# Two transformer layers in one kernel: the order of the first loads, and scales that TensorE spreads over the partitions

## What is computed

```python
x = x + fake_quant(layernorm(x)) @ fake_quant(ctx)      # uint8 grids, ctx is 2 x 1024 x 1024
x = x + attention0(layernorm(x))                         # 32 heads, 8 key/value heads, rotary, biases bq, bk, bv
x = x + experts0(layernorm(x))                           # 64 experts of rank 16, top 16
x = x + neighbours(ctx, layernorm(x))                    # 16 nearest of 1024 points, weights affine_w, affine_b
x = x + attention1(layernorm(x))                         # causal, output projection
x = x + experts1(layernorm(x))                           # 8 experts, top 1

def fake_quant(x, scale, zp):                            # scale and zp are one number each
    return (clip(round(x / scale + zp), 0, 255) - zp) * scale
```

## Time and profile before

| | |
|---|---|
| device time, median of 3 runs | 268.38 us (268.18 to 269.42) |
| the profiled execution's own time | 268.93 us |
| span of the profile, first to last instruction | 267.1 us |
| busy: PE / VectorE / ScalarE / GpSimd | 216.7 / 197.6 / 78.6 / 24.0 us |
| chain that ended last, share of the span | PE 47%, VectorE 31%, ScalarE 9%, transfers 4%, GpSimd 4% |
| bytes moved | 44.88 MB, 168 GB/s on average |

### The profile page before, as it was taken

How to read it: one execution, slowest core, us unless ns; L and a number is a source line. 1 busy time by engine, 2 the same in 40 slices (tenths; PEclk the granted TensorE clock), 3 DMA queues, 4 the chain that set the end, 5 groups by cost and what they waited for, 6 DMA issues and landing times.

```text
span 267.1 us, 4882 instructions
## 1 busy us (share of the span) xinstructions
PE 216.7 (81%) x2107; PEld 140.9 (53%) x2107; DVE 197.6 (74%) x356; ACT 78.6 (29%) x120; POOL 24.0 (9%) x34
## 2 busy tenths in 40 slices
PE   0419999899969398779966995698978999897983
PEld 0214447345758276564435444697966475654561
DVE  3759888999976999989999796958781135861433
ACT  1279962100282456545107103000001021430010
POOL 4155931000000000010000001000001000000010
PEclk9999999999997559599999999689999999999999
DMA  2699999980065059457739575000079000000002
GB/s 59 229 415 410 412 410 356 336 347 5 0 176 140 4 163 306 158 167 328 303 116 415 211 301 221 2 5 2 5 253 376 2 0 2 2 0 2 0 0 79
DMA packets 17435, 44.88 MB, mean 168 GB/s; under 512 B 2364, under 2 KB 7614, under 8 KB 16391
## 3 DMA queue, kind: packets, MB, share of 16 engines
q1 hardware_dynamic: 16256, 43.90, 45.2%
q10 hardware_dynamic: 1158, 0.69, 0.9%
HBM read 43.99 MB, written 0.59 MB: 167 GB/s over the span
## 4 chain that ended last, share of the span: by engine, by line
PE 47%; DVE 31%; ACT 9%; DMA 4%; POOL 4%; issue 3%; ACTq 1%; DVEq 0%; POOLq 0%; SPq 0%
PE banks L360 8%; PE banks L375 7%; PE banks L648 6%; PE banks L428 5%; PE banks L612 5%; ACT bufZ L688 4%; DVE bufY L1212 3%; POOL arc L1321 3%; DVE knn_d L938 3%; DVE idx L933 3%; DVE idx L946 3%; DVE v L942 3%; DMA ring<-in_ctx 3%; DVE v L929 3%; PE banks L287 3%
## 5 line engine op out<-in xcount | busy, mean ns | idle before, releaser
L287 PE MATMUL banks<-cst 128*128 128x256 bf16 (+1 forms) x182 | 22.2, 274 | 0.7 <-ACT arc L712 0.7
L360 PE MATMUL banks<-are,xnT 128*128 128x512 f32 (+1 forms) x64 | 21.7, 492 | 0.7 <-ACT xnT L816 0.7
L929 DVE MAX8 v<-banks 128x8 f32<-128x1024 f32 x16 | 19.5, 1219 | 3.0 <-PE banks L281 3.0
L287 PEld LDWEIGHTS banks<-cst 128*128 128x128 bf16 (+1 forms) x182 | 17.9, 103 | 6.3 <-issue 4.2
L1308 POOL TENSOR_SCALAR veps<-mv 128x1 f32<-128x1 f32 x6 | 1.3, 221 | 217.4 <-DVE mv L915 217.4
L816 ACT COPY xnT<-banks 128x512 f32<-128x512 f32 x8 | 4.3, 589 | 52.7 <-PE banks L300 52.7
L942 DVE MAX8 v<-knn_d 128x8 f32<-128x1024 f32 x16 | 19.6, 1223 | 0.2
L933 DVE FIND_INDEX8 idx<-v,banks 128x8 uint32<-128x1024 f32 x16 | 19.6, 1223 | 0.0
L317 PE MATMUL banks<-cst,ring 128*128 128x128 f32 x96 | 16.7, 331 | 3.5 <-ACT ard L712 2.9
L946 DVE FIND_INDEX8 idx<-v,knn_d 128x8 uint32<-128x1024 f32 x16 | 19.5, 1218 | 0.0
L1212 DVE COPY_PREDICATED bufY<-hi_mask,banks 128x256 f32<-128x256 uint8 (+1 forms) x40 | 15.3, 388 | 5.6 <-PE banks L648 4.4
(11 more groups left out here) (191 smaller groups left out, 357.0 us busy)
## 6 DMA issues: line engine op xcount, KB each, us to landing
ring<-in_ctx SPq DMA_DIRECT2D x4, 1024.0 KB, 9.9
are<-in_L_attn_wq SPq DMA_DIRECT2D x1, 4096.0 KB, 26.1
ring<-in_L_ffn_A SPq DMA_DIRECT2D x4, 1024.0 KB, 13.4
are<-lo_scratch SPq DMA_DIRECT2D x4, 1024.0 KB, 7.3
ard<-in_L_attn_Wq SPq DMA_DIRECT2D x1, 4096.0 KB, 13.9
ring<-lo_scratch SPq DMA_DIRECT2D x4, 1024.0 KB, 4.6
arc<-in_L_attn_Wo SPq DMA_DIRECT2D x1, 4096.0 KB, 13.8
ard<-in_ctx SPq DMA_DIRECT2D x3, 1024.0 KB, 16.5
```

Of the source, the lines that this page charges most:

```text
L287: mm(bank[bk][low:P, 0:2 * P], idle_pat[:, low:P], idle_pat[:, :], start=True, stop=True)
L360: m = mm(o, xnTk[:, k, :], w(k), start=(l == 1 and k == 0), stop=(k == KT - 1))
L929: v.max(v8[:, 0, :], dist_ps[:, :]).then_inc(sem("max_done"), 1)
```

## The change

Five edits. ScalarE issues the constants, x, and the four numbers, now each as a single element into a row of four on partition 0 (`scale_row`); the biases and the two affine loads move to SyncE, behind the context and ahead of the weights. SyncE queues the context when the constants have landed, and no longer waits for the points and the numbers. PE multiplies the row of ones by the row of four ahead of its first transposes, which puts the four numbers on all 128 partitions in PSUM, and VectorE copies them into `scal` before the quantiser's scalars. VectorE's order in the search changes: second_max(0), first_max(1) and second_index(0) come before the sums. The three `wsel` operations move from before the context product to after `advance(3)`.

```diff
--- before.py
+++ after.py
@@ -126,6 +126,7 @@
         veps = sb("veps", [P, 1])
         bperm = sb("bperm", [P, 2 * HALF])
         onesr = bufY[0:1, 1536:1536 + P]
+        scale_row = bufY[0:1, 1536 + P:1540 + P]
         xout = bufX[:, 0:D]
 
         ident = cst[:, C_ID:C_ID + P]
@@ -214,10 +215,13 @@
                 b, k, n = CHUNKS[i]
                 load(ctx_chunk(i).rearrange("p (k n) -> p k n", k=n), ctx_v[b, :, k:k + n, :], f"ld_ctx{i}")
 
-            sp.wait_ge(sem("ld_xy"), 32)
-            sp.wait_ge(sem("ld_scal"), 64)
+            sp.wait_ge(sem("ld_cst"), 16)
             for i in range(len(CHUNKS)):
                 load_ctx(i)
+            for n, (o, w) in (("L0_attn_bq", (0, D)), ("L0_attn_bk", (D, DKV)), ("L0_attn_bv", (D + DKV, DKV))):
+                load(bufY[0:1, o:o + w], A[n].unsqueeze(0), "ld_bias")
+            load(scal[:, 4:20], A["L1_xattn_affine_w"].partition_broadcast(P), "ld_affine")
+            load(scal[:, 20:21], A["L1_xattn_affine_b"].partition_broadcast(P), "ld_affine")
             for n, (o, w) in (("L0_attn_wq", (0, D)), ("L0_attn_wk", (D, DKV)), ("L0_attn_wv", (D + DKV, DKV))):
                 load(W0[:, :, o:o + w], A[n].rearrange("(k p) n -> p k n", p=P), "ld_" + n[-2:])
             sp.wait_ge(sem("ctx_quant"), 5)
@@ -529,6 +533,9 @@
                         dist(10)
 
 
+            pe.wait_ge(sem("ones_set"), 1)
+            pe.wait_ge(sem("ld_scal"), 64)
+            mm(bank[4][:, 0:4], onesr[:, :], scale_row, start=True, stop=True).then_inc(sem("scal_spread"), 1)
             pe.wait_ge(sem("ld_cst"), 16)
             pe.wait_ge(sem("feat_ones"), 3)
             pe.wait_ge(sem("feat_sq"), 2)
@@ -761,13 +768,9 @@
                 act.dma_start(dst, src).then_inc(sem(name), 16)
 
             load(cst[:, :], A["consts"], "ld_cst")
+            load(x[:, :], A["x"].rearrange("b s d -> (b s) d"), "ld_x")
             for i, n in enumerate(("L0_xattn_x1_scale", "L0_xattn_x1_zp", "L0_xattn_x2_scale", "L0_xattn_x2_zp")):
-                load(scal[:, i:i + 1], A[n].partition_broadcast(P), "ld_scal")
-            load(x[:, :], A["x"].rearrange("b s d -> (b s) d"), "ld_x")
-            for n, (o, w) in (("L0_attn_bq", (0, D)), ("L0_attn_bk", (D, DKV)), ("L0_attn_bv", (D + DKV, DKV))):
-                load(bufY[0:1, o:o + w], A[n].unsqueeze(0), "ld_bias")
-            load(scal[:, 4:20], A["L1_xattn_affine_w"].partition_broadcast(P), "ld_affine")
-            load(scal[:, 20:21], A["L1_xattn_affine_b"].partition_broadcast(P), "ld_affine")
+                load(scale_row[:, i:i + 1], A[n].unsqueeze(0), "ld_scal")
 
             def evac_points(b, i):
 
@@ -1073,7 +1076,8 @@
 
             def quantiser():
 
-                dve.wait_ge(sem("ld_scal"), 64)
+                dve.wait_ge(sem("scal_spread"), 1)
+                link(v.tensor_copy(scal[:, 0:4], bank[4][:, 0:4]))
                 v.reciprocal(sc2[:, 0:1], s1).then_inc(sem("scal_ready"), 1)
                 v.reciprocal(sc2[:, 1:2], s2).then_inc(sem("scal_ready"), 1)
                 v.tensor_scalar(sc2[:, 2:3], z1, -1.0, QMID, ALU.mult, ALU.add).then_inc(sem("scal_ready"), 1)
@@ -1106,18 +1110,16 @@
             first_max(0)
             first_index(0)
             take_out(0)
+            second_max(0)
+            first_max(1)
+            second_index(0)
             dve.wait_ge(sem("xn_ready"), 2)
             sums()
-            advance(0)
+            first_index(1)
+            take_out(1)
             advance(1)
             second_max(2)
             first_max(3)
-            dve.wait_ge(sem("ld_cst"), 16)
-            dve.wait_ge(sem("ld_affine"), 32)
-            link(v.tensor_tensor(wsel[:, 0:16], cst[:, C_SELK:C_SELK + NN], scal[:, 4:20], ALU.mult))
-            link(v.tensor_reduce(sc2[:, 8:9], wsel[:, 0:16], AX.X, ALU.add))
-            v.tensor_scalar(wsel[:, 16:24], cst[:, C_SELJ:C_SELJ + 8], sc2[:, 8:9], None, ALU.mult)\
-                .then_inc(sem("wsel_ready"), 1)
             for b in range(NB):
                 dve.wait_ge(sem("xattn0_filled"), b + 1)
                 o = S * b
@@ -1141,6 +1143,12 @@
             first_index(3)
             take_out(3)
             advance(3)
+            dve.wait_ge(sem("ld_cst"), 16)
+            dve.wait_ge(sem("ld_affine"), 32)
+            link(v.tensor_tensor(wsel[:, 0:16], cst[:, C_SELK:C_SELK + NN], scal[:, 4:20], ALU.mult))
+            link(v.tensor_reduce(sc2[:, 8:9], wsel[:, 0:16], AX.X, ALU.add))
+            v.tensor_scalar(wsel[:, 16:24], cst[:, C_SELJ:C_SELJ + 8], sc2[:, 8:9], None, ALU.mult)\
+                .then_inc(sem("wsel_ready"), 1)
             attention(0, [[4], [5], [6]], [8, 9])
             normalise(2, parts=4)
             advance(10)
```

## The result

The change makes the kernel faster, by less than was forecast. Over 22 runs of each, the changed kernel has a median of 267.59 us and the kernel before 270.24; the ratio is 0.9896, with a 95% interval of 0.9866 to 0.9925. That is a gain of 1.04% (0.75 to 1.34%), 2.8 us, where 3.8 us (ratio 0.986) were forecast. The median lies 0.3 us above the range on record, and 3.0 us above the forecast of 264.6. Of these, 1.9 us are the kernel before, which came out higher in many runs (270.24) than in the three on which the sum was based (268.38); the other 1.1 us are missing gain.

A forecast was written before the change was run, and what follows sets the result against it. It took the start to be bound by two transfers in sequence, last scale then context. ScalarE 3.9 to 4.1 us earlier, less about 0.2, gave 3.8: median 268.38 to 264.6 us, range 263.6 to 267.3.

The forecast's parts named there:

- Gate of the context: Start: context queued at about 3.1 instead of 6.95 us, first chunk landing between 8.1 and 9.9; broadcast descriptors called slow.
- Scales: Start: four scales land at 5.9 us, spread by PE and hidden beside VectorE's features except for VectorE's copy.
- Rival 1: Late scales: landing at 7.35 to 8.8 us, gain 3.0 to 1.5, time 265.4 to 266.9; chance 0.18.
- What ScalarE must have done first: Before the first quantisation: row copy from 8.63 to 9.63 us, so quantisation at 9.66, or 9.9 with the old chunk time.
- the term of VectorE's cast: Start: VectorE's cast of the right half done at 6.41 us, after which PE's transposes could run from 6.66.
- The middle: Search and sums: VectorE's new order stalls PE 0.4 us, given back, then 0.1 us on the chain; cost 0.1 us.
- rival 2: Gain given back later, through VectorE's order or slack: up to about 2.5 us lost, time 265.5 to 267.8; chance 0.13.
- Between the projection and the scores: After the first projection at about 44.1 us: VectorE's wait before the scores stays near 3.6 us.
- Selection operations, small loads, weights: Selection operations behind advance(3) and small loads ahead of the weights: no cost, with 4.6 us of slack for the weights.
- Sum: Whole kernel: ScalarE 3.9 to 4.1 us earlier, less 0.1 for distances and about 0.1 for waits: 3.8 us gained.
- The range: Median of the changed kernel: 263.6 us (early chunk, shorter later waits) to 267.3 us, reaching into the gain-given-back case.
- Rival 4: Slower by PE's clock: low level on PE-bound work costs one more per microsecond; 8 us give 272.6; chance 0.06.

The follow-up runs named there:

- gate_only: Kernel before with one edit: SyncE queues the context when the constants have landed, scales still broadcast; ratio 0.9923 to the kernel before.
- order_only: Kernel before with only VectorE's new order of the search and the sums; ratio 1.0049 to the kernel before.
- x_last: Changed kernel with x issued after the four numbers; ratio 0.9952 to the kernel before.
- gap_fill: Changed kernel with the sums ahead of first_max(1) in VectorE's idle time and 12 filler matmuls ahead of the first scores; ratio 0.9876 to the kernel before.
- after_again: The changed kernel run once more, unaltered, on the chip and in the rounds of three other kernels; ratio 0.9915 to the kernel before.
- one_input: Changed kernel with the last two operations of the sums using one tensor input and a per-partition scalar, same place; ratio 0.9852 to the kernel before.

## Why the prediction was wrong, step by step

- *Gate of the context:* right. Queued at 2.99 (3.1 said); the chunk took 5.2 us, near the low bound of 5.0, and 4.9 to 6.2 in the seven traces with x first. It was not last, as the sum had it. The reason given, slow broadcasts, fits these traces (6.8 before, 8.3 in gate_only, with broadcasts ahead), but no run changes only them.
- *Scales:* right. On PE at 5.52 (5.9 said), hidden. Rival 1 did not come.
- *What ScalarE must have done first:* the term of VectorE's cast was mis-sized. It was taken over as done at 6.41; it was 7.14, since the points landed 0.73 us later: x, issued ahead of the numbers, filled the transfer engines at 266 to 380 GB/s from 2 to 4 us. Quantisation at 10.22 instead of 9.66: 0.56 us of the gain.
- *The middle, "cost of the new order: 0.1 us":* this step failed. It measured 1.2 us at the projection. The sums were priced at 2.3 us from the old trace and took 3.3. Two of the three have two inputs in SBUF and can wait for GpSimd: at the old place one of them had paid 0.66 us for it, where nobody waited; at the new place the other paid 1.7. PE's stall was forecast at 0.4 us and taken to be given back; it was 1.49, and since take_out(2) was late as well, only some 0.3 us were given back. This is rival 2, which had 0.13.
- *Between the projection and the scores:* the sum took the shift to pass through unchanged, and had no term for the clock there. In the changed kernel it nearly did (2.34 and 2.25). But it would not have at the size forecast: the three kernels without PE's wait were 3.5 to 3.7 us ahead of the kernel before at the projection and 2.3 to 2.9 at the scores. So even a free new order would have left the gain short of 3.8 us, and of the 1.2 us only 0.1 to 0.7 would have come through.
- *Selection operations, small loads, weights:* right, at nothing each.
- *Sum:* 3.8 forecast. By the marks 3.53 at the quantisation, 2.34 at the projection, 2.25 at the scores. The measured ratio gives 2.8, with 2.0 to 3.6 by its interval. The 3.6 us of the profiled pair are near the forecast by luck, by the 1.3 us of chance above.
- *The range:* the sum started from three runs at 268.38. With 270.24, the same forecast reads 266.4 with a range of 265.5 to 269.2. So the new order alone does not carry the median out of the range; the low base does most of it. The variation from run to run (265.3 to 271.9 us for the changed kernel) was not in the range, and should have been.
- *Rival 4:* ahead of the projection not in the changed kernel's profile, but order_only, x_last and gap_fill show the mechanism at 3 to 4 us of low clock in a PE-bound stretch, for 1.4 to 1.7 us each.

## What to carry to other kernels

When an operation is moved, its duration does not move with it: look in the old trace for operations far longer than their size explains, see with what they end, and ask who will be running at the new place. A small VectorE operation on two SBUF tensors beside a busy GpSimd can often be written with one tensor and a per-partition scalar. When small loads are what the first operations wait for, count the large ones that are issued beside them.

## What the runs showed of the hardware that was not expected

- A VectorE operation of 128x1 with two SBUF inputs took 1.86 us (five traces) and ended with GpSimd's conversion; the same numbers with one tensor input took 0.21 us beside the same conversion (one_input).
- The same code had full clock in some executions and 3 to 4 us of the lower level in others. With one wait of 1.5 us on PE in a stretch filled with dummy matmuls, two traces had full clock (changed, after_again) and two a low stretch, at once (order_only) or some 13 us later (x_last); gap_fill had that later stretch without the wait.
- The first chunk, issued 2.99 to 3.46 us into the kernel, took 4.9 to 6.2 us to land with x ahead of it (seven traces) and 6.1 to 7.7 with x issued just before it (four traces).
